# A decoder layer on one core: weigh pairs behind the second score of a row, a token tile ahead of bulk transfers, low parts ahead of a SiLU

## The reference

```python
x = x + attention(layernorm(x))          # 16 heads of 32, rotary positions, causal softmax
x = x + cross(layernorm(x), ctx)         # softmax(q k^T) over 512 features, mixed into the tokens
x = x + ffn(layernorm(x))                # shared SwiGLU (704 wide) + top 2 of 8 experts (352 wide each)
```

## Time and profile before

| what | value |
|---|---|
| median of 3 runs | 1038.44 us (1037.35 to 1039.83) |
| the profiled execution's own time | 1036.79 us |
| span of that execution, first to last instruction | 1034.7 us |
| PE busy | 974.4 us (94%) |
| DVE, ACT, POOL busy | 614.0, 486.0, 182.9 us |
| mean granted PE clock | 0.990 |

### The profile page before, as it was taken

The page is one execution under the profiler, slowest core; times in us unless marked ns, Lnnn a source line. Parts: engine busy times, 40 slices in busy tenths (PEclk is TensorE's granted clock), DMA queues, the critical chain, the costliest instruction groups (busy, mean ns, idle before and its releaser), DMA issues.

```text
span 1034.7 us, 18246 instructions
## 1 busy us (share of the span) xinstructions
PE 974.4 (94%) x6186; PEld 780.9 (75%) x6186; DVE 614.0 (59%) x1621; ACT 486.0 (47%) x1276; POOL 182.9 (18%) x209
## 2 busy tenths in 40 slices
PE   8988999899998999998699999999999999999998
PEld 6456666667666676665567798888898889889997
DVE  5698777776876767767244657344433442444565
ACT  1568765656646566568533231244433443342221
POOL 3221211211112211110000001011111111112342
PEclk9999999999999999999989999999999999999999
DMA  9665744448444573374800031744434434424564
GB/s 238 107 104 69 152 97 63 62 64 248 87 53 63 78 218 66 48 149 147 288 25 21 23 110 33 255 152 136 135 124 149 161 103 136 153 72 125 173 193 150
DMA packets 69835, 124.88 MB, mean 121 GB/s; under 512 B 6336, under 2 KB 22720, under 8 KB 69760
## 3 DMA queue, kind: packets, MB, share of 16 engines
q1 hardware_dynamic: 63296, 104.76, 40.4%
q0 software_dynamic: 5600, 18.35, 6.0%
q10 hardware_dynamic: 864, 0.79, 0.5%
HBM read 70.14 MB, written 28.57 MB: 95 GB/s over the span
## 4 chain that ended last, share of the span: by engine, by line
PE 75%; DVE 9%; ACT 5%; DMA 4%; issue 3%; SPq 2%; POOL 0%; DVEq 0%; ACTq 0%; POOLq 0%
PE ps L1341 22%; PE ps L1351 11%; PE ps L1104 8%; PE ps L1253 5%; PE ps L1195 5%; PE ps L1156 5%; PE ps L1179 3%; PE ps L1143 3%; PE ps L1129 3%; DVE gu_lo L1664 2%; PE ps L1359 2%; PE ps L1046 2%; PE ps L1329 1%; DMA routed_x<-xn_d,table_cur 1%; DMA ks<-rope_a 1%
## 5 line engine op out<-in xcount | busy, mean ns | idle before, releaser
L1514 DVE CUSTOM_DVE_ANT_0 probs<-ps,mask 128x128 f32<-128x128 f32 (+3 forms) x256 | 122.8, 486 | 80.3 <-PE ps L1143 40.5
L858 ACT COPY probsT<-ps 128x128 f32<-128x128 f32 (+3 forms) x256 | 109.0, 427 | 117.5 <-PE ps L1156 116.6
L850 ACT ACTIVATE probs<-probs,nb 128x128 f32<-128x128 f32 (+3 forms) x256 | 146.9, 574 | 25.2 <-DVE nb L1519 24.9
L1143 PE MATMUL ps<-ks,qs 96*128 96x256 f32 (+2 forms) x256 | 126.2, 500 | 12.9 <-DVE mx L1514 11.0
L1156 PE MATMUL ps<-ident,probs 128*128 128x128 f32 x640 | 113.9, 279 | 5.2 <-ACT probsT L858 3.2
L960 ACT ACTIVATE sg<-ps 128x352 f32<-128x352 f32 x69 | 32.0, 464 | 174.9 <-PE ps L1341 174.7
L1798 DVE TENSOR_TENSOR hidden<-sg,ps 128x352 f32<-128x352 f32 x69 | 35.8, 519 | 118.7 <-ACT sg L960 118.7
L1156 PEld LDWEIGHTS ps<-ident,probs 128*128 128x128 f32 x640 | 79.9, 143 | 32.4 <-issue 21.6
L1802 DVE TENSOR_TENSOR h_lo<-ps,h_hi 128x384 fp32r<-128x384 f32 x69 | 38.5, 557 | 84.4 <-ACT h_hi L964 84.4
L1351 PE MATMUL ps<-d_hi,h_hi 128*128 128x512 f32 (+1 forms) x207 | 86.6, 418 | 1.3 <-DVE h_lo L1802 1.3
L1143 PEld LDWEIGHTS ps<-ks,qs 96*128 96x128 f32 x256 | 49.6, 194 | 45.5 <-DVE mx L1514 20.9
(11 more groups left out here) (187 smaller groups left out, 2080.9 us busy)
## 6 DMA issues: line engine op xcount, KB each, us to landing
gu_raw<-in_we SPq DMA_DIRECT2D x10, 1408.0 KB, 6.8
y_d<-y_sb SPq DMA_DIRECT2D x37, 256.0 KB, 2.4
shared_x<-xT_d SPq DMA_DIRECT2D x32, 256.0 KB, 2.8
qs<-rope_b SPq DMA_DIRECT2D x30, 256.0 KB, 5.7
ks<-rope_b SPq DMA_DIRECT2D x30, 256.0 KB, 5.2
d_raw<-in_we SPq DMA_DIRECT2D x10, 512.0 KB, 7.7
attT<-in_wpT SPq DMA_DIRECT2D x4, 1024.0 KB, 8.5
acc<-in_x SPq DMA_DIRECT2D x4, 1024.0 KB, 10.6
```

The lines of the kernel that those rows point to most:

```text
L850: nc.scalar.activation(pr, pr, ACT.Exp, bias=nb[:, n % 2, h:h + 1], scale=SCALE, accum_out=sums[:, n % 2, h:h + 1]).then_inc(exp_done, 1)
L858: nc.scalar.copy(probsT[n % 2][:, h, 0:w], ps[:, T_BANK + h % 2, 0:w]).then_inc(pT_done, 1)
L1143: nc.tensor.matmul(ps[:, S_BANK + h % 2, 0:w], stacks[G % 2][0][:, h, i * P:(i + 1) * P], stacks[G % 2][1][:, h, 0:w], start=True, stop=Tr ...
L1514: nc.vector.tensor_tensor_reduce(probs[n % TT][:, h, 0:w], ps[:, S_BANK + h % 2, 0:w], mask[:, TOKENS - w:], 1.0, LOWEST, ALU.add, ALU.max ...
```

## The change

It moves work; no product is added or removed. Six edits go together:

- `weigh` of a pair of rows is done at h = 1 of a row right behind `scores(r, 1)`, instead of last at h = 0; `turn_probs(·, 0)` no longer waits behind it.
- SP: for the last batch `load_projection` is issued at place 254 instead of 259, `load_residual` after the store of the turned tiles; then `load_tokens(1)`, the second part of `acc`, and only then `load_weights(1)`.
- ACT loads the table of the SiLU behind `turn(shared, 1)` instead of ahead of the shared places.
- In each routed block the four gate and up chunks are split ahead of the first tile's SiLU (ACT) and product (DVE); the two down chunks stay behind.
- The first piece of the attention weights is split at place 28 instead of 37, all low parts are made two places behind the high part instead of one; batch 1's first norm is turned one place later; the second norm's scaling is spread to places 36, 37, 40 and 41.
- `turn_first(b, 0)` for batches 2 and 3 no longer waits for the rotary products; only tile 1 does.

```diff
-SPLIT_WEIGHTS = (37, 46, 52, 57, 70, 78)
+SPLIT_WEIGHTS = (28, 46, 52, 57, 70, 78)
...
-FIRST_LN1 = dict(LN1, stats=(22, 25, 27, 29), variance=(31,), scale=(33, 34, 35, 36))
+FIRST_LN1 = dict(LN1, stats=(22, 25, 27, 29), variance=(31,), scale=(33, 34, 35, 36), turn=(40, 41, 42, 43), copy=(40, 41, 42, 43),
+                 low=(41, 42, 43, 44))
...
-    second_stats=(23, 31, 31, 32), second_variance=(33,), second_scale=(36, 36, 37, 38), second_turn=(40, 41, 42, 43),
+    second_stats=(23, 31, 31, 32), second_variance=(33,), second_scale=(36, 37, 40, 41), second_turn=(40, 41, 42, 43),
...
-                if at == RESIDUAL and 0 < b <= BATCHES:
+                if at == RESIDUAL and 0 < b < BATCHES:
                     load_projection(b - 1)
                     load_residual(b - 1)
+                if place == LAST_PROJECTION:
+                    load_projection(BATCHES - 1)
...
+            load_residual(BATCHES - 1)
+            load_tokens(1)
+            sp.dma_start(acc[:, 2 * TT:RES, :], mixed_v[:, 2 * TT:RES, :]).then_inc(acc_loaded, 16)
             load_weights(1)
-            sp.dma_start(acc[:, 2 * TT:RES, :], mixed_v[:, 2 * TT:RES, :]).then_inc(acc_loaded, 16)
-            for j in range(1, BEFORE_LAST + 1):
+            for j in range(2, BEFORE_LAST + 1):
                 load_tokens(j)
...
-            nc.scalar.activation(silu_unused[:], bias_sb[:, 0:1], ACT.Silu)
...
                     turn(shared, j + 1)
+                    if j == 0:
+                        nc.scalar.activation(silu_unused[:], bias_sb[:, 0:1], ACT.Silu)
...
+                act.wait_ge(raw_loaded, (e + 3) * RAW)
+                split(e + 2, e % 2, range(CC))
                 silu(routed, lo)
...
-                split(e + 2, e % 2)
+                split(e + 2, e % 2, range(CC, WC))
...
-                    pe.wait_ge(rope_raw, 2 * unit(GROUPS * b - 1, t if b == 1 else 1) + 2)
-                    if b >= 2:
+                    if b == 1 or t == 1:
+                        pe.wait_ge(rope_raw, 2 * unit(GROUPS * b - 1, t if b == 1 else 1) + 2)
+                    else:
                         pe.wait_ge(aT_done, (b - 2) * TT + 3)
...
+                ready = step_at(place, WEIGH_LAG)
+                if h == 1 and ready is not None and ready % 2 == 1:
+                    weigh(ready - 1)
+                    weigh(ready)
...
-                if place - 1 in SPLIT_WEIGHTS:
-                    weight_low(SPLIT_WEIGHTS.index(place - 1))
+                if place - 2 in SPLIT_WEIGHTS:
+                    weight_low(SPLIT_WEIGHTS.index(place - 2))
...
+                for i in range(CC):
+                    low_part(e + 2, e % 2, i)
                 gate_by_up(routed, lo)
...
-                for i in range(WC):
+                for i in range(CC, WC):
                     low_part(e + 2, e % 2, i)
```

More of the change, by code:

```diff
@@ L621, in _ @@
             RAW_X, RESIDUAL, LOAD_ACC = 8, 3, (BATCHES - 1) * PLACES + 48
+            LAST_PROJECTION = (BATCHES - 1) * PLACES + 62
             FIRST_TOKENS = (BATCHES - 1) * PLACES + 56
@@ L941, in attend, with split @@
                     high_part(0, 0, SPLIT_PLACES.index(place))
-            def split(n, buf):
-                act.wait_ge(raw_loaded, n * RAW + RAW)
-                for i in range(WC):
+            def split(n, buf, parts):
+                for i in parts:
                     high_part(n, buf, i)
@@ L1299, in attend @@
                         turn_inverse(n, r - TURN_LAG)
-                ready = step_at(place, WEIGH_LAG)
-                weighs = h == 0 and ready is not None and ready % 2 == 1
                 turned = step_at(place, TURN_LAG)
-                if turned is not None and not weighs:
+                if turned is not None:
                     turn_probs(turned, h)
@@ L1318, in attend @@
                 cross(place)
[L1319 to L1323, removed]
             def turn(path, j):
```

## The result

| | before | after |
|---|---|---|
| median | 1038.38 us (1036.78 to 1042.47, 20 runs) | 1032.09 us (1027.29 to 1039.93, 20 runs) |
| ratio after to before [95% interval] | | 0.9942 [0.9927, 0.9957] |
| profiled execution, its own time | 1036.79 us | 1030.51 us |
| PE busy | 974.4 us | 975.6 us |
| mean granted PE clock | 0.990 | 0.988 |

The change makes the kernel 0.6% faster, 6.3 us. The forecast of 1025.6 us had the direction right, and a size of 12.8 us, about double what was measured.

The account below looks back on a forecast made before the run. PE was taken as the bound (94% busy). Terms -11.0 + 5.3 - 2.5 - 3.1 - 1.5 = -12.8 took the profiled 1036.8 to 1024.0 us, 1025.6 us for the median; range 1013 to 1035 us.

Parts of the forecast that it names:

- Start of the shared expert: Wait ahead of the first `turn_hidden`: token tile 1 lands earlier, PE resumes 8.6 us sooner; -11.0 us with the clock.
- The drain: SiLU table load on ACT: with the skill's drain of about 1380 ns, the start's gain would be 1.0 us less.
- the half-clock stretch behind the long idle time: Shared expert's start, 518 to about 522.8: 4.9 us of work at half speed, expected to go, worth 2.4 us.
- Rival 2: Shared expert's start: tile 1 still lands after about 507, the start gives -6, total 1030.6 us; chance 0.12.
- Start of each routed block: Early low parts save 1.0 us per block, but the load released earlier delays a gather to 6.8 us; sum +5.3 us.
- Rival 1: Routed blocks: the gather shares the queues, stays at about 4.5 us, no new stall; 1013.3 us; chance 0.2.
- Batch 0: Attention: the 1.7 us wait for `rope_b` and 1.7 us of half clock go, 1.2 us added; -2.5 us.
- Batches 1 and 2: Attention: tile 0 turned without the rotary wait, tile 1 1.55 us sooner, twice; -3.1 us.
- the pairs: Attention, weighing pairs of rows: the waits for `inverseT`, 1.9 us, mostly go; -1.5 us (bounds +2, -4).
- the term of the half-clock stretches: Stretches removed counted as gain: 2.4 us at the shared expert's start, 1.7 us in batch 0; none added.
- rival 3: Routed blocks: the new gather stall drops PE's clock, up to +10.2, 1035.8 us; chance 0.13, of which 0.03 slower.
- Rival 4: Attention: reordered pairs stall ACT, +2 instead of -1.5, and batch 0 gives +1.2; 1032.8 us; chance 0.05.

Follow-up runs that it names:

- run 1: The changed kernel with the raw weight load issued behind each block's first stored tile: 1022.09 us, ratio 0.9847 to the kernel before.
- run 11: The changed kernel with each block's first tile stored, then the load, then the other stores: 1018.72 us, ratio 0.9809 to the kernel before.
- run 12: The changed kernel with the load in two parts, gate and up behind the block's first store, down behind the second: 1015.71 us, ratio 0.9765 to before.
- run 9: The kernel before once more, unchanged, profiled: 1036.78 us, span 1034.6.
- run 8: The kernel before with only batch 0's tables and batch 1's first norm changed: 1039.32 us, ratio 0.9998.
- run 2: The changed kernel without the routed blocks' edit (all splits behind the first tile, as before): 1019.90 us, ratio 0.9838 to the kernel before.
- run 3: The kernel before with only the routed split changed: 1052.10 us, ratio 1.0131.
- run 10: The changed kernel once more, unchanged, profiled: 1032.77 us, span 1030.6.
- run 6: The kernel before with only the pairs weighed at h = 1: 1035.80 us, ratio 0.9983.
- run 4: The kernel before with only SP's reordered transfers and the SiLU table's new place: 1030.24 us, ratio 0.9908.
- run 7: The kernel before with only the second norm's scaling spread and tile 0's wait for the rotary product dropped: 1034.81 us, ratio 0.9977.
- run 5: The kernel before with only SP's transfer order changed, the SiLU table loaded where it was: 1028.09 us, ratio 0.9904.

## Why the prediction was right in part

*Start of the shared expert: right but for the clock.* The idle time fell from 10.04 to 1.40 us, 8.6 as forecast. Tile 1 was there 8.5 us ahead of the end of PE's second product, where the forecast had 5.9. What is late next is the second energy's maximum, as forecast; ACT's turn, table and SiLU came in the order and at the durations given, and the SiLU ended at 502.16, 0.16 us behind PE's second product (0.5 forecast). The drain of "ScalarE: Activation LUTs" in the Trainium skill does not show: the table took 1.28 us and nothing idled behind it. Tile 2, `acc` and the weights cost nothing: no wait for them stands in the list. The 2.4 us for the half-clock stretch behind the long idle time did go, but a stretch at 483.0 came in the same stage (some 1.7 us), which leaves 9.1 us between place 252 and shared tile 1; and one more stretch stands among the shared tiles (623.0), whose time grew by 1.3 us. Rival 2 did not come: tile 1 was there in time.

*Start of each routed block: the mechanism and the stall right.* The low parts ahead of the product save 1.1 us in seven blocks (1.0 forecast): the block's first tile takes 6.72 instead of 7.84 us. The load goes ahead of the gather by 2 us, and six gathers take 5.9 to 7.6 us (6.8 forecast); PE idles 1.94 us for one (2.1 forecast). In the profile the stage grew by 8.9 us; less two half-clock stretches (3.4) that is 5.5, against +5.3 (in which block 7 stands with 1.3 us saved, though 1.0 was worked out for each; it measured 1.1). Runs 1, 11 and 12 show that it is the place of the load: with it later, the same edit of ACT and DVE loses the stalls. Rival 1 failed here: a gather with the load ahead of it lands 2.4 to 4.1 us later than the median of 3.5. By "DMA: Bandwidth & Descriptors", Arbitration, of the Trainium skill, queues take turns packet by packet; these six landings do not fit its mild form. The packets in the traces show where most of the delay lies: the first packet of these six gathers starts 4.1 to 4.3 us after the issue, against 1.7 us for nearly all other gathers of this trace. In run 11 it starts after 3.0 to 3.3 us, and in run 12 after 1.7. Why it starts late no run shows.

*Batch 0: two steps wrong, the size open.* I priced -2.5. The idle time was taken as removed, though DVE's next product was late too, so a wait of 1.67 us came at 84.17; what went is the second wait of 1.27 us, which run 9 shows. And the half-clock stretch was priced at 1.7 us, though run 9 shows 0.1, since PE waits for DVE right behind it with either clock. By the time run 8 gave 0.2 us (between 1.9 gained and 1.5 lost), by its trace 1.3 us or more in batch 0.

*Batches 1 and 2, and the pairs: right within what can be told.* -3.1 and -1.5 were forecast; alone they measured 2.4 us, with an interval that nearly reaches zero, and 1.8, with one that includes it. Together the attention gave 6.8 us in the profile, against 7.1 for all three of its terms.

*The sum, and the step that failed: the clock.* Without it the terms were -8.6, +5.3, -0.8 (batch 0 less its 1.7), -3.1 and -1.5, -8.7 us together. The profile, freed of 1.7 us for each stretch of 3.4 and of 2.4 for the long one, moved by -10.8: the span by -6.4, with 7.5 us lost to half speed before and 11.9 after (an upper figure for the stretches in the attention, by run 9). I had set the clock at -4.1, as two stretches removed and none added; in this pair of profiles it was +4.4. The granted clocks of all executions say the same less sharply. The span times one minus the mean clock is 12.3 us in 51 executions of before and 12.6 in 20 of after. About 2.7 us of the first is half of the idle time inside the long stretch (10.2 us in all six traces without the new order of transfers), which was no work. What work lost to the lower clock so went from 9.6 to 12.6 us, +3.0 where I had -4.1, and all the rest, by the means, moved by -9.2 where I had -8.7. The step that failed is thus the term of the half-clock stretches: those removed were counted in full as gain, and the new stalls of the routed stage were charged with none. Run 2 shows the second part with nothing else changed: without the stalls the clock is 0.9928 instead of 0.9878, 5.2 us. This is rival 3, which I gave 0.13 as a case apart from the forecast. Runs 3, 9 and 10 show why that was wrong: a stall of 2 us is followed by the lower clock in some executions and not in others, so six of them bring some of it each time (two, three and three of the six in the traces of after, run 3 and run 10). Rival 4 did not come (run 6).

What stays open: the parts do not add up exactly. Runs 4, 6, 7, 8 and 3 sum to -0.3 us by their ratios (their intervals together some 4.6 us either way), the change gave -6.0; without run 3 they sum to -13.9, and run 2 gave -16.8. The mean granted clock differs from part to part: 0.9927 in run 4, 0.9860 in run 6, 0.9861 in run 7, 0.9867 in run 8 and 0.9833 in run 3, against 0.9881 before. Between executions of after the time goes from 1027.3 us at a mean granted clock of 0.991 to 1039.9 at 0.981 (correlation -0.92 over 20 runs), so a few microseconds between kernels can be such stretches. Why one idle time is followed by the lower clock and its like is not was not settled.

## What to carry to other kernels

When an engine off the path is made faster, follow it to the transfer that it releases: here low parts done 3 us sooner (the load is issued 3.8 us into the block's first tile instead of 7.0) put a 2 MB load in front of a 256 KB gather, and the edit cost 12 us; with the load issued in two parts behind two stores, the same kernel was the fastest of all. A small transfer that something waits for goes ahead of bulk ones, at the start of the shared expert as in each block. And a half-clock stretch in one profile is no fixed cost: ask whether the engine would wait right behind it anyway, and charge new stalls of 2 us with a share of it, before counting a removed one as gain.

## What the runs showed of the hardware

- The same program has the lower clock behind other idle times in each execution: of four stretches in the first trace of before two (at 82.5 and 447.7) are missing in the second, and one at 685.5 is new; the idle times themselves agree within 0.1 us.
- Stretches at half clock also stand where PE had been busy: in after at 585.4, with no idle time of 0.2 us or more in the 25 us ahead of it.
- In the trace of after, a gather lands 5.9 to 7.6 us after its issue when a 2112 KB load leads it by 2 us, 5.3 to 6.3 when it leads by 4.3 us (run 11), 3.3 to 5.8 when 1408 KB lead by 4.3 us and 704 KB are issued behind the next store (run 12); the median of all gathers of these three traces is 3.4 to 3.5. Its first packet starts 4.1 to 4.3 us after the issue in the first case, 3.0 to 3.3 in the second and 1.7 in the third.
- A table load of ACT took 1.28 us in every place read, and where the next instruction had nothing to wait for (the loads from 494 to 530 in before, after and runs 4 and 5) it began within 0.03 us of its end.
